# Cross-attention and feed-forward block on one core: another order for the first three tiles' products, and tile 3's transposes between them

## The reference

```
h   = rmsnorm(layernorm(x), g_res) @ W_in.T + b_in        # 512 -> 512
x   = x + h + depool(rmsnorm(ctx, g_init), mask)          # a scan over 3202 context rows, gathered by the mask
h   = gelu(layernorm(x) @ w1 + b1)                        # 512 -> 2048
x   = x + h @ w2 + b2                                     # 2048 -> 512
```

## Time and profile before

| | us |
|---|---|
| median of 3 runs | 831.86 (831.57 to 832.02) |
| the profiled execution | 834.93 |
| its span on the core | 833.2 |
| TensorE (PE) busy | 822.3 (99% of the span) |
| VectorE busy | 315.9 (38%) |
| ScalarE busy | 294.0 (35%) |
| POOL busy | 258.0 (31%) |

### The profile page before, as it was taken

How to read it: one execution, slowest core, us unless ns; L and a number is a source line. 1 busy time by engine, 2 the same in 40 slices (tenths; PEclk the granted TensorE clock), 3 DMA queues, 4 the chain that set the end, 5 groups by cost and what they waited for, 6 DMA issues and landing times.

```text
span 833.2 us, 10703 instructions
## 1 busy us (share of the span) xinstructions
PE 822.3 (99%) x3722; PEld 675.9 (81%) x3722; DVE 315.9 (38%) x513; ACT 294.0 (35%) x542; POOL 258.0 (31%) x238
## 2 busy tenths in 40 slices
PE   7999999999999999999999999999999999999998
PEld 5877878788888888888888888888888888888886
DVE  5899852665141423233332423143113411241112
ACT  5668446422622253224422262222222222222221
POOL 2254659940633035301630062305300250011000
PEclk9999999999999999999999999999999999999999
DMA  9988994260236022602233113302300240010001
GB/s 227 281 263 282 291 301 153 89 163 22 68 102 160 0 76 88 167 7 74 72 113 80 50 58 103 50 0 101 51 1 1 79 72 0 0 50 1 1 0 51
DMA packets 39057, 78.11 MB, mean 94 GB/s; under 512 B 6369, under 2 KB 6369, under 8 KB 37265
## 3 DMA queue, kind: packets, MB, share of 16 engines
q1 hardware_dynamic: 30052, 65.95, 24.3%
q0 software_dynamic: 4608, 8.39, 6.4%
q10 hardware_dynamic: 4368, 3.42, 1.5%
HBM read 51.02 MB, written 22.84 MB: 89 GB/s over the span
## 4 chain that ended last, share of the span: by engine, by line
PE 81%; POOL 7%; DVE 4%; DMA 3%; issue 2%; SPq 1%; ACT 1%; ACTq 0%; POOLq 0%; DVEq 0%
PE acc L889 13%; PE acc L890 13%; PE acc L891 13%; PE h_bank L889 13%; PE h_bank L890 13%; PE h_bank L891 13%; DMA xa_odd<-in_x_dram 2%; POOL w_lo L545 2%; PE t_bank L948 2%; POOL x_cur L651 1%; POOL x_next L577 1%; DMA scan_table<-cl_next 1%; POOL cl L564 1%; POOL w_lo L551 1%; DVE h_lo L1070 1%
## 5 line engine op out<-in xcount | busy, mean ns | idle before, releaser
L1303 DVE TENSOR_TENSOR h_lo<-g_f,h_hi 128x512 fp32r<-128x512 f32 x128 | 101.1, 790 | 432.1 <-ACT g_f L826 432.1
L824 ACT ACTIVATE h_hi<-h_bank,b_c 128x512 fp32r<-128x512 f32 x128 | 87.9, 687 | 429.5 <-PE h_bank L891 425.9
L889 PE MATMUL h_bank<-xt_hi,w_hi 128*128 128x512 f32 x512 | 199.9, 390 | 0.6 <-POOL w_lo L545 0.6
L889 PE MATMUL acc<-w_hi,h_hi 128*128 128x512 f32 x512 | 199.8, 390 | 0.0
L891 PE MATMUL h_bank<-xt_hi,w_lo 128*128 128x512 f32 x512 | 199.3, 389 | 0.0
L890 PE MATMUL h_bank<-xt_lo,w_hi 128*128 128x512 f32 x512 | 199.2, 389 | 0.0
L891 PE MATMUL acc<-w_hi,h_lo 128*128 128x512 f32 x512 | 199.2, 389 | 0.0
L890 PE MATMUL acc<-w_lo,h_hi 128*128 128x512 f32 x512 | 199.2, 389 | 0.0
L889 PEld LDWEIGHTS h_bank<-xt_hi,w_hi 128*128 128x128 f32 x512 | 96.1, 188 | 20.7 <-issue 1.0
L891 PEld LDWEIGHTS h_bank<-xt_hi,w_lo 128*128 128x128 f32 x512 | 96.1, 188 | 20.0
L891 PEld LDWEIGHTS acc<-w_hi,h_lo 128*128 128x128 f32 x512 | 96.1, 188 | 20.0
(11 more groups left out here) (168 smaller groups left out, 701.1 us busy)
## 6 DMA issues: line engine op xcount, KB each, us to landing
out_dram<-x_cur SPq DMA_DIRECT2D x32, 256.0 KB, 2.1
x_next<-x_part SPq DMA_DIRECT2D x7, 1024.0 KB, 5.0
w_raw<-in_L_ffn_w_dram SPq DMA_DIRECT2D x6, 1024.0 KB, 9.0
scan_table<-cl SPq DMA_DIRECT2D x6, 896.0 KB
ch<-in_ctx_dram SPq DMA_DIRECT2D x20, 256.0 KB, 2.9
cl<-in_ctx_dram SPq DMA_DIRECT2D x5, 1024.0 KB
xa_odd<-in_x_dram SPq DMA_DIRECT2D x16, 256.0 KB, 7.3
x_part<-xa_odd SPq DMA_DIRECT2D x16, 256.0 KB, 3.9
```

What stands on the lines that cost most here:

```text
L824: act.activation(h_hi[:, m % HB, :], h_bank[m % 2][:], ACT.Gelu, bias=b1_c[:, m:m + 1])
L889: nc.tensor.matmul(dst, a_hi, b_hi, start=first, stop=False)
L1303: dve.tensor_tensor(h_lo[:, m % HB, :], g_f32[:], h_hi[:, m % HB, :].bitcast(F32), ALU.subtract).then_inc(h_split, 1)
```

## The change

TensorE's instruction stream before the fourth tile is written anew; no other engine's is. `project_first_part` becomes `project_late_part` and serves slices 2 and 3 alone. For slices 0 and 1 the three products of a part are issued apart: `by_high_w_in` (both halves of x by the high half of W_in; it waits for the high half of the slice and the low half of the tile), `by_low_w_in` (waits for the low half of the slice), and for tile 2 `both_of_x` (the high half of x by both halves of W_in) and `low_of_x`. The transposes of tile 3 stand after tile 0's first five products.

```
-            for k in (0, 1):
-                project_first_part(0, k)
-                project_first_part(1, k)
-            project_first_part(2, 0)
-            project_first_part(2, 1)
+            by_high_w_in(0, 0)
+            by_low_w_in(0, 0)
+            by_high_w_in(0, 1)
             transpose_first(3)
+            by_high_w_in(1, 0)
+            by_low_w_in(1, 0)
+            by_high_w_in(1, 1)
+            by_low_w_in(0, 1)
+            by_low_w_in(1, 1)
+            both_of_x(2, 0)
+            both_of_x(2, 1)
+            low_of_x(2, 0)
+            low_of_x(2, 1)
             for k in (2, 3):
                 for t in range(3):
-                    project_first_part(t, k)
+                    project_late_part(t, k)
```

```
+            def by_high_w_in(t, k):
+                c = slice(k * P, (k + 1) * P)
+                pe.wait_ge(win_hi_done, k + 1)
+                pe.wait_ge(x_lo, t + 1)
+                nc.tensor.matmul(p_bank[t % 3][:], h_hi[:, t % HB, c], win_hi[:, k, :], start=(k == 0), stop=False)
+                nc.tensor.matmul(p_bank[t % 3][:], h_lo[:, t % HB, c], win_hi[:, k, :], start=False, stop=False)
+
+            def by_low_w_in(t, k):
+                c = slice(k * P, (k + 1) * P)
+                pe.wait_ge(win_lo_done, k + 1)
+                nc.tensor.matmul(p_bank[t % 3][:], h_hi[:, t % HB, c], win_lo[:, k, :], start=False, stop=False)
+
+            def both_of_x(t, k):
+                pe.wait_ge(x_hi, t + 1)
+                pe.wait_ge(win_lo_done, k + 1)
...
+            def low_of_x(t, k):
+                pe.wait_ge(x_lo, t + 1)
...
-            def project_first_part(t, k):
+            def project_late_part(t, k):
                 pe.wait_ge(x_lo, t + 1)
-                if k < 2:
-                    pe.wait_ge(win_lo_done, k + 1)
-                else:
-                    pe.wait_ge(win_lo_late, k - 1)
+                pe.wait_ge(win_lo_late, k - 1)
                 project_part(t, k)
```

## The result

| | before | after |
|---|---|---|
| median | 831.88 us (831.28 to 834.59, 22 runs) | 835.12 us (832.66 to 837.44, 22 runs) |
| profiled execution | 834.93, span 833.2 | 834.84, span 833.1 |

The change makes the kernel slower: by 3.2 us in the medians, and by 2.4 us by the ratio over all runs, 1.0029 (95% interval 1.0021 to 1.0036, which is 1.7 to 3.0 us). The median is outside the predicted range, which ended at 833.3. The two profiled executions, 834.93 and 834.84, show no difference at all. So the first thing to find was which trace is the unusual one. From here on "the usual trace of before" is that one.

The account below looks back on a forecast made before the run. TensorE was taken to bound the kernel. TensorE -1.01, taken back by +1.01 more waiting at 50.1, and +0.4 from tile 10's load took the profiled 834.93 to 835.3, the median 831.86 to 832.3 us; range 831.0 to 833.3.

Parts of the forecast that it names:

- TensorE 0.81 sooner at the late part, 1.01 in all: TensorE's start: late part 0.81 us sooner, plus 0.20 from the wait at 26.93 gone, 1.01 us ahead.
- Nothing of it reaches the end: At the end, TensorE's 1.01 us gain counts 0, taken back by more waiting for VectorE at 50.1.
- the waits at 50.1 and 57.7: TensorE's waits for VectorE's low halves: 0.51 growing to 1.52 us at 50.1, 0.69 as before at 57.7.
- ScalarE's issues and q10's data sooner: ScalarE's DMA queue: issues 2.5 to 2.9 us sooner, at 15.5 to 15.95; q10's data 1.5 us sooner.
- The start behind the backlog: DMA queues: q10's data starts only behind q1's backlog, some 627 packets, so 1.5 us sooner; gives +0.4 us.
- the rivals with a start at 16.1 or 20.6: q10's data start: 16.1 by the skill page, +0.69 us; 20.6 if 5.1 us is fixed, nearly all 0.69.
- Tile 10 later by 0.4: Tile 10's load on q1: q10's earlier packets go ahead of it and make it land 0.4 us later.
- VectorE's chain from it stays: VectorE behind tile 7's low half at 33.80: the chain stays unchanged and holds TensorE first at 50.1.
- The base: Whole kernel: the forecast difference on the profiled 834.93 us was applied to the median 831.86, giving 832.3.
- The price of 0.179 us for a packet of q1 ahead of 22: DMA engines before 22: 0.179 us a packet, against 0.082 for q10's later; at most 3.1 us later landing.
- The slower rival: DMA engines before 22.0: q10's packets turn slow and hold tile 10 back, +1.5 to +3.1 us; chance 0.10.

Follow-up runs that it names:

- the usual trace of before: The unedited kernel before, traced a second time; its profiled execution took 832.01 us, close to its median.
- f3: Changed kernel with VectorE's mask work moved two steps earlier, ahead of tile 10's landing: 830.40 us, 0.9977 of the kernel before.
- f4: Kernel before with VectorE's mask work moved two steps earlier, ahead of tile 10's landing: 831.68 us, ratio 0.9993.
- f1: Changed kernel again, unedited: 835.18 us, 1.0033 of the kernel before.
- f2: Changed kernel with POOL waiting for g_init's load alone ahead of its products, not all four of ScalarE's loads: 833.92 us, 1.0022 of the kernel before.
- n1: Changed kernel with POOL's first three context products cut to one column of 512: 831.94 us, 0.9993 of the kernel before.
- e2: Kernel before's product order with only tile 3's transposes moved up: 833.74 us, 1.0005 of the kernel before.
- e3: Changed kernel with ScalarE's four DMA issues put behind the statistics of tile 6: 834.57 us, 1.0013 of the kernel before.
- r3: Repeat of e3, the changed kernel with ScalarE's four DMA issues behind tile 6's statistics: 834.63 us, 1.0028 of the kernel before.
- s1: Changed kernel with SyncE's store of tile 4 and the loads behind it held until tile 10 has landed: 834.09 us, 1.0023 of the kernel before.
- s2: Changed kernel with SyncE's store of tile 4 and following loads held until all four of ScalarE's loads have landed: 833.93 us, 1.0022 of the kernel before.
- k1: Changed kernel with POOL waiting on g_init alone and ScalarE's other three loads issued at tile 9's step: 830.37 us, 0.9981 of the kernel before.
- e1: Changed kernel's product order with tile 3's transposes back at their old place: 833.22 us, 1.0001 of the kernel before.
- r2: Repeat of e1, the new product order with tile 3's transposes at their old place: 832.97 us, 1.0015 of the kernel before.
- n2: Kernel before with POOL's first three context products cut to one column of 512: 831.05 us, ratio 0.9986.

## Why the prediction was wrong, point by point

- *TensorE 0.81 sooner at the late part, 1.01 in all*: right. 0.82 measured; 1.28 between f3 and f4, where no low half behind tile 4's is waited for.
- *Nothing of it reaches the end*: right for the kernel as it is. In the changed kernel the reason is the one given: TensorE stands 3.3 us for VectorE's low halves, against 1.4 in the earlier trace rows. But in the usual trace of before it is 0.2: the waits at 50.1 and 57.7, on which the step rested, belong to the slower execution, and there only the 0.2 by which VectorE's chain was ahead could have been gained. The changed kernel's timeline of TensorE has the waits at three places, the first of which I had not foreseen:

```profile
42.95 0.50 PE L889 MATMUL acc<-win_hi,h_hi 128*128 128x512 f32 x1 [1.48 <-DVE h_lo L1100]
...
50.71 0.50 PE L889 MATMUL h_bank<-win_hi,h_hi 128*128 128x512 f32 x1 [1.09 <-DVE h_lo L1100]
...
58.33 0.50 PE L889 MATMUL acc<-win_hi,h_hi 128*128 128x512 f32 x1 [0.70 <-DVE h_lo L1100]
```

  The 1.48 is three collisions ahead of it and takes TensorE's whole lead at once; 1.5 had been forecast for the second and 0.69 for the third.
- *ScalarE's issues and q10's data sooner*: issues at 15.04, 3.4 us sooner than in the earlier trace rows, 3.0 once the earlier start of 0.37 is taken off; 2.5 to 2.9 had been forecast. The high half of tile 3 started at 15.57 and ScalarE idled 5.14 ahead of tile 10, where 16.0 and over 4.23 had been named. q10's first data came 1.8 sooner than in the usual trace of before (21.1 against 22.9), where 1.5 had been worked out from the backlog of q1. q1 moved about 685 packets between issue and q10's first data in the changed kernel and 643 in the usual trace of before, against the 627 of the prediction. The start behind the backlog held, and the rivals with a start at 16.1 or 20.6 fall.
- *Tile 10 later by 0.4*: about 0.9. It lands at 31.0 to 31.8 in seven traces with early transposes and the store as it falls (after, f1, f2, n1, e2, e3, r3), at 29.5 to 30.3 in all without them but the first trace of before. (f3, whose store goes out late, s1, s2 and k1 are told apart.) The size was off, and so was the cause: e3 and r3 issue when e1 and r2 do, and only in e3 and r3 does tile 10 land late.
- **The step that failed: "VectorE's chain from it stays".** I had carried the low half of tile 7 to the wait at 57.7 as a block of fixed length. From the low half of tile 7 to that of tile 13 it is 22.4 us long in the usual trace of before, 23.2 in the one that I read and 24.3 in the changed kernel: it contains operations that are stopped by POOL, and which ones are stopped depends on when POOL's products start, which hangs on ScalarE (third collision) and on the landing of b1 (fourth). I had priced b1 only as traffic ahead of tile 10, never by who waits for it: POOL's wait for all four loads stood in no step of mine.
- *The base*: the trace that I read was an execution of 834.93 with n = 3 and a landing at 31.47. I scaled its differences to the median of 831.86 as if the kernel were the same in both. In the usual execution VectorE's chain ends just ahead of TensorE's own stream: with the chain shortened, the kernel before gains no more than 0.3 to 0.8 in the medians (f4, n2). Of the 2.9 us by which the trace that I read was longer 2.4 were on that chain (1.4 landing, 1.0 a collision), and I took them for a fixed part of it. The range, made from one chain's spread, was too narrow for that. The price of 0.179 us for a packet of q1 ahead of 22 was of that execution too: in the usual trace of before q1 moved 922 packets in 14:22 at 106.0%, 0.147 each.
- The slower rival (833.4 to 835.0) comes near the right size by a wrong mechanism: q10's packets did not get dear ahead of 22. In the changed kernel 82 of them went there at 5.7% of 8 us, 0.089 each and not 0.179.

**What stays open.** Why tile 10 lands some 0.9 later when tile 3's transposes are early. It isn't the moment of ScalarE's issues (e3, r3). In the traces with early transposes where SyncE's store of tile 4 goes out only behind the landing, it is sooner again in two (s2 30.03, f3 30.21) and hardly in the third (s1 30.80), which speaks for that store with one reserve; and s2's median lies 1.0 above its own trace, and 0.7 above what one collision makes of before, which speaks against it. A part of the spread is no part of the change: from 14 to 21 us q1 moved 652 packets in the first trace of before and 644 in f2 and n1, against 706 to 781 in all others, and these three have the latest landings, 31.46 to 31.77. What made q1 slower there isn't known. How often each number of collisions occurs can't be told from single traces either.

**A better version.** h4, the changed order with the mask work early, POOL's own semaphore and late small loads, is at 830.22, 0.27% below the kernel before (0.9973, 0.9963 to 0.9983), in the range expected. TensorE waits there for the first slice of W_in and 0.6 for POOL:

```profile
PE acc L922 <- ACT win_hi L762: 1.2, 1, 1.2
PE h_bank L894 <- POOL w_lo L546: 0.6, 1, 0.6
```

The mask work alone (f3, 0.9977), or POOL's own semaphore and the late loads (k1, 0.9981), give the same within the intervals.

## What to carry to other kernels

A chain of engine work between two waits isn't a constant: look in it for short operations that are shown several times their usual length, ask what ran beside them on POOL, and what releases that, since a lead won elsewhere can move one onto the other. A semaphore shared by several loads makes its waiter as late as the slowest of them, here a load of 8 KB that its waiter didn't need. And before differences are put on a median, look whether the profiled execution is near it; if it is 3 us off, its critical chain may be another one.

## What the runs showed of the hardware

- VectorE's short operations, 0.17 to 0.19 us, take up to 1.3 us when they start beside a 128x512 product of POOL (1.3 us), and end within 0.05 us of its end. It hits operations with two inputs (L1161) and with one (L1138, L1140) alike; the trace counts the stop as busy.
- A load of 2048 pieces of four bytes (8 KB) took 13.9 us from issue to landing in the usual trace of before and 19.9 in the changed kernel. With SyncE's store and loads held back until tile 10 had landed (s1) it took 17.6, from an issue as early as in the changed kernel.
- ScalarE's first DMA moved no data for 6 us after its issue at 15.04 (5.1 for that at 18.41, 4.3 for that at 18.55 in the usual trace of before), while loads that SyncE had queued before took 104 to 107% of the 16 engines.
